# Layer-2 probabilities from a second score product with the keys on the partitions, with an order written out for each engine

## The reference

```python
# layer 0
alpha = max((x@wq) @ (x@wk).T, 0) * (adj != 0);  alpha = softmax(alpha, axis=1)
y = layernorm(x + alpha @ (x@weight))
# layer 1, per head
q, k, v = heads(y@Wq + bq), heads(y@Wk + bk), heads(y@Wv + bv)
scores = where(adj == 0, -inf, q @ k.T / sqrt(32))
attn = softmax(scores, axis=-1)
out = layernorm(y + (attn @ v) @ Wo + bo)
```

## Time and profile before

| what | value |
|---|---|
| median of three runs | 2967.55 us |
| the profiled execution, its own time | 2969.42 us |
| its span (first to last instruction) | 2967.6 us |
| mean granted PE clock | 0.992 |
| PE busy | 2902.2 us, 98% |
| DVE busy | 2365.3 us, 80% |
| ACT busy | 2016.6 us, 68% |
| POOL busy | 582.6 us, 20% |
| DMA, mean busy share of the 16 engines | 23.3% for the kernel's queue |

### The profile page before, as it was taken

How to read it: one execution, slowest core, us unless ns; L and a number is a source line. 1 busy time by engine, 2 the same in 40 slices (tenths; PEclk the granted TensorE clock), 3 DMA queues, 4 the chain that set the end, 5 groups by cost and what they waited for, 6 DMA issues and landing times. The chain is left out here.

```text
span 2967.6 us, 65967 instructions
## 1 busy us (share of the span) xinstructions
PE 2902.2 (98%) x24264; PEld 1775.5 (60%) x24264; DVE 2365.3 (80%) x4627; ACT 2016.6 (68%) x6414; POOL 582.6 (20%) x1289
## 2 busy tenths in 40 slices
PE   7899999999999999999999999999999999999996
PEld 4565666656666656666666666666666666666554
DVE  4588888888888788888788888888888888888886
ACT  3476676666676766676767766767776766776665
POOL 1121122121122121121121221121221211221210
PEclk9999999999999999999999999999999999999997
DMA  3222122222122222122221122221122221222220
GB/s 121 61 72 76 43 56 73 57 76 72 37 65 61 69 76 62 40 72 54 76 76 54 48 72 54 76 76 47 51 76 54 76 76 42 57 71 59 75 53 24
DMA packets 96369, 188.06 MB, mean 63 GB/s; under 512 B 18608, under 2 KB 34992, under 8 KB 96048
## 3 DMA queue, kind: packets, MB, share of 16 engines
q1 hardware_dynamic: 96048, 183.84, 23.3%
HBM read 49.55 MB, written 33.55 MB: 28 GB/s over the span
## 5 line engine op out<-in xcount | busy, mean ns | idle before, releaser
L647 ACT ACTIVATE e<-sm,nmax 128x128 f32<-128x128 f32 x2048 | 791.1, 391 | 27.6 <-DVE nmax L776 25.6
L598 ACT ACTIVATE qk<-front,bqk 128x512 f16<-128x512 f32 x256 | 175.9, 687 | 381.6 <-PE front L429 381.6
L825 POOL TENSOR_TENSOR ln<-ln 128x1 f32<-128x1 f32 x256 | 49.0, 192 | 1890.2 <-DVE ln L804 1496.6
L647 ACT ACTIVATION_READ_ACCUMULATOR e<-sm,nmax 128x1 f32 x2048 | 391.0, 191 | 0.0
L664 DVE SCALAR_TENSOR_TENSOR pT<-pt_bank,pT 128x512 f16<-128x512 f32 x512 | 348.9, 681 | 42.6 <-ACT pT L653 42.1
L653 ACT ACTIVATE pT<-pt_bank 128x512 f16<-128x512 f32 x512 | 302.8, 591 | 103.6 <-PE pt_bank L543 101.6
L776 DVE TENSOR_REDUCE nmax<-sm 128x4 f32<-128x512 f32 x512 | 351.3, 686 | 17.7
L429 PE MATMUL fin_bank<-W_O,oT 128*128 128x512 f16 x1536 | 356.3, 382 | 1.4 <-DVE oT L664 1.4
L429 PE MATMUL front<-W_V,yT 128*128 128x512 f16 x1536 | 354.0, 380 | 0.0
L429 PE MATMUL front<-xT,W_A 128*128 128x512 f16 x1536 | 353.6, 380 | 0.3 <-DVE xT L664 0.3
L429 PE MATMUL front<-yT,W_Q 128*128 128x512 f16 x1536 | 352.2, 379 | 1.6 <-DVE yT L664 1.6
(11 more groups left out here) (111 smaller groups left out, 4482.3 us busy)
## 6 DMA issues: line engine op xcount, KB each, us to landing
q_st<-qk SPq DMA_DIRECT2D x384, 128.0 KB, 2.4
k_st<-qk SPq DMA_DIRECT2D x384, 128.0 KB, 2.4
x_sb<-in_x SPq DMA_DIRECT2D x128, 256.0 KB, 3.4
out_x<-z_sb SPq DMA_DIRECT2D x128, 256.0 KB, 2.5
adj_i<-in_adj SPq DMA_DIRECT2D x32, 256.0 KB, 4.6
y_sb<-in_L_gnn_wq SPq DMA_DIRECT2D x1, 1024.0 KB, 5.6
yb<-in_L_gnn_wk SPq DMA_DIRECT2D x1, 1024.0 KB, 8.1
x_p<-in_L_gnn_weight SPq DMA_DIRECT2D x1, 1024.0 KB, 10.5
```

Source lines behind the costliest of these rows:

```text
L598: i = act.activation(dst, src, ACT.Identity, bias=bias, scale=scale)
L647: act.activation(e1[:, k % 2, h, :], sm[:, k % SM_BUFS, h, :], ACT.Exp, bias=nmax[:, k % SM_BUFS, h:h + 1], accum_out=esum[:, n % 2, head: ...
L825: pool.tensor_tensor(ln[:, 8:9], ln[:, 7:8], ln[:, 8:9], ALU.add).then_inc(moments, 1)
```

## The change

- **Probabilities.** `exp`, `pT` and the transposes of the probabilities go. The scores are computed twice. `S` as before (queries on the partitions) now only serves the row maxima: DVE takes a minimum with a mask of huge values (`smin`) and the negated maxima (`smax`), in two steps. When the four quads of a graph are through, `m` transposes the 16 columns of maxima (one PE transpose f32), ACT and DVE write their HI and LO parts (16 partitions x 128), and SP copies each part into one more row of `q_st` (`m_stack`, 2 DMAs for a graph, rows 96 and 97); `k_st` has a constant in these rows. `T` is the second product, with keys on the partitions, 98 rows: its result is the score minus the row's maximum, already transposed. DVE adds a lift and takes a minimum with a transposed mask; ACT takes the exponential twice over the whole quad, once as f16 (HI) and once as f32; POOL subtracts (`lo`, LO). `PV` follows directly; v has a column of ones beside each head, so its 33rd column is the row sum. `pv_bank` is two banks by halves of eight heads (`o_inv`, `o` in halves).
- **Masks** are made by POOL (`maskb`, `maskT`) instead of DVE. The `mask_size` steps go.
- **x.** ACT and POOL first write the parts of x, then PE transposes these, eight f16 transposes for a job, into a bank read as f16; DVE copies 128x1024 f16 in one instruction. ACT has no part in `xT` any more.
- **Stacking.** The columns of W_Q and W_K are permuted so that q and k come out with head r of a quad interleaved; 12 DMAs of 256 KB a group, three for each operand and pair of quads, and `S` waits for each pair alone.
- **Banks.** `m`, `oT` and `fin` share one bank (`tail`); `adjT` is one job.
- **Order.** Each engine has a list of its own (`ORDER`). `<` is a group's lag, `>` a lead. Dependent DVE instructions are steps of their own, with others between. There is no order of its own for the end: passes −2 to groups+3 run the same list and leave out what does not exist.

```diff
-def pass_order():  ...  (one list for all engines; removed with age, order, drain_order)
+ORDER = {
+    "PE": """
+        fin.0<< yT.1< T.7<< S.12<< yT.2< m.2<< v.0< S.13<< yT.3< PV.5<< PV.6<< xT.0 S.14<< T.8<< xT.1 k.0< S.15<<
+        T.9<< PV.7<< k.1< m.3<< T.10<< PV.8<< q.0< T.11<< PV.9<< q.1< xT.2 T.12<< PV.10<< q.2< T.13<< q.3< oT.1<<
+        T.14<< PV.11<< k.2< PV.12<< xT.3 T.15<< k.3< fin.1<< PV.13<< S.0< t.0 t.1 oT.2<< S.1< t.2 PV.14<< PV.15<< S.2<
+        t.3 S.3< adjT.0 v.1< S.4< m.0< alpha.0 S.5< alpha.1 fin.2<< S.6< T.0< v.2< T.1< S.7< oT.3<< v.3< T.2< z.0 z.1
+        PV.0< S.8< m.1< PV.1< T.3< z.2 z.3 S.9< fin.3<< PV.2< g.0 T.4< PV.3< S.10< g.1 T.5< oT.0< S.11< g.2 g.3 T.6<
+        yT.0 PV.4<
+    """,
...
+    "DVE": """
+        xT.1 o_inv.3<< m.3<< k.0< T.10<< T.11<< k.1< z_bn.0<< o.3<< q.0< z_ag.0<< T.12<< o_inv.4<< xT.2 q.1< T.13<<
+        o.4<< q.2< T.14<< q.3< xT.3 oT.1<< k.2< o_inv.5<< T.15<< k.3< o.5<< z1.1<< smin.0< z_bn.1<< adj01.0 smin.1<
+        t.0 o_inv.6<< t.1 z_ag.1<< o.6<< oT.2<< o_inv.7<< smax.0< smax.1< smin.2< t.2 smax.2< smin.3< t.3 smax.3<
+        adjT.0 o.7<< smin.4< m.0< v.1< smin.5< alpha.0 smax.4< a_max.0 alpha.1 a_max.1 smax.5< z1.2<< p_inv.0 T.0<
+        p_invp.0 p_inv.1 smin.6< p_invp.1 z_bn.2<< smax.6< z_ag.2<< p_lo.0 p_lo.1 smin.7< p_lo.2 T.1< p_lo.3 v.2<
+        oT.3<< smax.7< T.2< v.3< z.0 smin.8< m.1< T.3< z.1 z.2 z.3 smin.9< o_inv.0< smax.8< o.0< smax.9< z1.3<< y.0
...
+    """,
+    "SP": """
+        stack_k.1<< store.0<<< store.1<<< m_stack.0<< m_stack.1<< load.0 load.1 load.2 store.2<<< load.3 m_stack.2<<
+        load_adj.0 m_stack.3<< store.3<<< stack_k.0< stack_q.0< stack_q.1<
+    """,
+}
# PE
                 if what == "xT":
+                        pe.wait_ge(xhi_ready, (g + 1) * GB)
+                        pe.wait_ge(xlo_ready, (g + 1) * GB)
+                    parts = bank[:, :].bitcast(F16)
+                    for part in (HI, LO):
+                        for n in range(GB):
+                            mm = pe.transpose(parts[:, at:at + P], x_p[:, part, n, k * P:(k + 1) * P], ident16[:, :])
-                elif what == "pT":
-                    for h in range(4):
-                        mm = pe.transpose(pt_bank[:, h * P:(h + 1) * P], e1[:, k % 2, h, :], ident[:, :])
+                elif what == "m":
+                    pe.wait_ge(nmax_ready, g * STEPS + QUADS * (k + 1))
+                    pe.transpose(tail[:, 0:P], nmax[:, k % 2, :], ident[:, :]).then_inc(m_full, 1)
+                elif what == "T":
+                    if quad == 0:
+                        pe.wait_ge(m_stacked[n], (g + 1) * 32)
+                    wait(pe, u_ready, g * STEPS + k)
+                    for h in range(4):
+                        mm = pe.matmul(t_bank[:, h * P:(h + 1) * P], k_st[0:ROWS, h, quad, n * P:(n + 1) * P],
+                                       q_st[0:ROWS, h, quad, n * P:(n + 1) * P], start=True, stop=True)
# ACT
-                    for h in range(4):
-                        act.activation(e1[:, k % 2, h, :], sm[:, k % SM_BUFS, h, :], ACT.Exp,
-                                       bias=nmax[:, k % SM_BUFS, h:h + 1], accum_out=esum[:, n % 2, head:head + 1])
-                    act.activation(pT[:, k % 2, HI, :], pt_bank[:, :], ACT.Copy, scale=P1_SCALE)
+                    act.activation(pT[:, k % 2, HI, :], src, ACT.Exp, scale=SCORE_UNSCALE).then_inc(phi_ready, 1)
+                    act.activation(e32[:, k % 2, :], src, ACT.Exp, scale=SCORE_UNSCALE).then_inc(e_ready, 1)
+                elif what == "m":
+                    act.activation(mT[:, k % 2, HI, :], tail[0:HEADS, 0:P], ACT.Copy, scale=M_SCALE)
# DVE
-                    lo_part(pT[:, k % 2, LO, :], pt_bank[:, :], P1_SCALE, pT[:, k % 2, HI, :])
+                elif what == "T":
+                    dve.scalar_tensor_tensor(out=u[:, k % 2, :, :], in0=t_bank[...], scalar=LIFT,
+                                             in1=maskT[:, n, :]..., op0=ALU.add, op1=ALU.min).then_inc(u_ready, 1)
+                elif what == "xT":
+                    dve.tensor_copy(xT[:, :, k, :], front_bank(what, k, g)[:, :].bitcast(F16)...)
# POOL
+                elif what == "lo":
+                    pool.tensor_tensor(pT[:, k % 2, LO, :], e32[:, k % 2, :], pT[:, k % 2, HI, :], ALU.subtract)
# SP
-                for r in range(4):
                     for row, part in enumerate(parts):
-                        sp.dma_start(dst[row * DH:(row + 1) * DH, r, :, :], qk[r * DH:(r + 1) * DH, n, part, :, :])
+                        sp.dma_start(dst[row * DH:(row + 1) * DH, :, pair, :], qk[:, n, part, pair, :])
+                elif what == "m_stack":
+                    for part, ready in ((HI, mhi_ready), (LO, mlo_ready)):
+                        sp.wait_ge(ready, g * GB + k + 1)
+                        sp.dma_start(q_st[MAXROWS + part:MAXROWS + part + 1, :, :, k * P:(k + 1) * P],
+                                     mT[:, k % 2, part, :]).then_inc(m_stacked[k], 16)
```

More of the change, by code:

```diff
@@ L100, in age @@
[L100 to L127, removed]
-    out = []
[L129 to L134, removed]
-    return out
@@ L139 @@
[L139 to L158, removed]
+MROW = 65504.0
+M_SCALE = 1.0 / MROW
@@ new lines, with steps_of, program @@
+FRONT = ("xT", "adjT", "t", "alpha", "z", "g", "yT", "q", "k", "v")
+BY_ACT = ("t", "z", "yT", "q", "k", "v")
+TAIL = ("m", "oT", "fin")
+def steps_of(engine):
+    out = []
+    for word in ORDER[engine].split():
+        name = word.rstrip("<>")
+        what, k = name.split(".")
+        out.append((what, int(k), word.count("<") - word.count(">")))
+    return out
+def program(engine, groups):
+    out = []
+    for p in range(-2, groups + 4):
+        for what, k, age in steps_of(engine):
+            if 0 <= p - age < groups:
+                out.append((what, k, p - age))
+    return out
@@ L263, in graph_layers @@
         y_ready = sem("y_ready")
[L264 to L268, removed]
+        maskb_ready = sem("maskb_ready")
+        maskT_ready = sem("maskT_ready")
+        stacked = [[sem(f"stacked_{n}{half}") for half in range(2)] for n in "qk"]
         yb_ready = sem("yb_ready")
@@ L272, in graph_layers @@
         nmax_ready = sem("nmax_ready")
[L273 to L276, removed]
+        mhi_ready = sem("mhi_ready")
+        m_full = sem("m_full")
+        mlo_ready = sem("mlo_ready")
+        m_stacked = [sem(f"m_stacked{n}") for n in range(GB)]
+        t_full = sem("t_full")
+        u_ready = sem("u_ready")
+        phi_ready = sem("phi_ready")
+        e_ready = sem("e_ready")
+        p_ready = sem("p_ready")
         pv_done = sem("pv_done")
@@ L294, in wait @@
         def wait(eng, s, value):
-            if not (isinstance(value, int) and value <= 0):
+            if value > 0:
                 eng.wait_ge(s, value)
[L299 to L309, removed]
@@ L408, in _ @@
[L408 to L420 removed]
+            for n, b in enumerate((bq, bk)):
+                for t in range(KT):
+                    sp.dma_start(bqk[:, n, t:t + 1], b[t * P:(t + 1) * P].rearrange("(r d) -> d r", r=4),
+                                 allow_slow_non_contiguous=True).then_inc(bias_loaded, 16)
@@ L425, in _, with split_product @@
         def _(pe):
-            def split_product(bank, left, right, k, of, last_inc=None):
+            def split_product(bank, left, right, k, of):
                 for n, (a, b) in enumerate([(HI, HI), (HI, LO), (LO, HI)]):
@@ L478, in step @@
                     if k == 0:
-                        pe.wait_ge(f_free, jobs_done(g, "xT", KT - 1))
-                    bank = bank_for(g)
+                        for n in range(KT):
+                            wait_freed(pe, "xT", n, g)
                     for t in range(KT):
@@ L485, in step @@
                     if k == 0:
-                        pe.wait_ge(f_free, jobs_done(g, "t", KT - 1))
-                    bank = bank_for(g)
+                        for n in range(KT):
+                            wait_freed(pe, "t", n, g)
                     for n in range(2):
@@ L502, in step @@
                     if k == 0:
-                        pe.wait_ge(f_free, jobs_done(g, "z", KT - 1))
-                    bank = bank_for(g)
+                        for n in range(KT):
+                            wait_freed(pe, "z", n, g)
                     for t in range(KT):
@@ L515, in step @@
                     if k == 0:
-                        pe.wait_ge(f_free, jobs_done(g, "yT", GB - 1))
-                    bank = bank_for(g)
+                        for n in range(GB):
+                            wait_freed(pe, "yT", n, g)
                     w = W_Q if what == "q" else W_K
@@ L712, in step @@
-                    dve.wait_ge(f_free, jobs_done(g, what, k))
+                    wait_freed(dve, "adjT", 0, g)
+                    dve.scalar_tensor_tensor(out=two(e0[:, pair, :]), in0=front_bank(what, k, g)[:, 0:2 * P], scalar=0.0,
```

(4 more changed lines are left out.)

646 lines of the change are left out of this document (330 added, 316 removed), and 18 rows, old and new, of the table LATE_ATTENTION.

## The result

| | before | after |
|---|---|---|
| median | 2968.16 us (2967.03 to 2969.31, 4 runs) | 3056.33 us (3055.15 to 3076.05, 4 runs) |
| span of the profiled execution | 2967.6 us | 3054.1 us |
| start to the first product of `t` | 39.2 us | 52.5 us |
| from there to the end of the last k projection | 2843.2 us | 2911.2 us |
| from there to the end | 85.2 us | 90.4 us |

The ratio is 1.0313, interval 1.0271 to 1.0354: the changed kernel is slower by 3%, where 2882 us was forecast and 2943 was the upper end of the range. Of the 86.5 us between the spans, 68.0 arose in the middle, 13.3 at the start and 5.2 at the end.

The account below looks back on a forecast made before the run. PE was taken as the bound, before and after. From the median 2967.55 us, −87 for 31 steady passes, +6 at the start and −5 at the end gave 2881.5, say 2882 us; range 2857 to 2943.

Parts of the forecast that it names:

- rival 4: In `xT`: f16 transposes cost the f32 price, +1.7 us a pass, 54 us in all, 2936 us; chance 0.05.
- 0.9 us of gaps: PE's idle time allowed per steady pass, in place of 0.4, for three tight hand-overs; turned −3.3 into −2.8 us.
- The sum: Whole kernel: −87 us over 31 steady passes, +6 at the start, −5 at the end, giving 2882 us.
- The tightest place: Row maxima to `T`: 3.5 to 4.0 us needed, against 4.5 us of PE work behind m.2.
- Rival 1: Late maxima: small copies land after 4.6 us for 2.4, m.2 1.6 us late; +61 us, 2943 us; chance 0.15.
- rival 3: POOL's subtractions lock DVE out of shared SBUF ports, lengthening the softmax chain; 2898 us, at worst 3009; chance 0.07.
- The start: Before the first `t` product: x's split 5.3 us later, bias loads 0 to 2 us; +6 us taken.
- Rival 2: Lost clock: `T` waits 2.93 us each pass, then PE slows by 1.4 us; 3000 us, chance 0.09.

Follow-up runs that it names:

- C: Copies alone, no other part of the kernel: 3.1 MB as 12 x 256 KB, 128 partitions to 32, runs of 2 KB, as in the kernel after; 26.6 us.
- e2: Kernel after with `T` reading weights instead of the stacked operands, so stacking waits for `S.15` alone; 2866.71 us, ratio to before 0.9653.
- v1: Whole change, but W_Q and W_K unpermuted and stacking in 24 copies of 128 KB a group, 32 partitions to 32; 2848.72 us, ratio to before 0.9598.
- e1: Kernel after, each operand's third stacking copies cut to 32 KB from the second group on; 2855.18 us, ratio to before 0.9619.
- b1: Kernel before with only the new stacking copies, 12 x 256 KB from 128 partitions onto 32, W_Q and W_K unpermuted; 3209.49 us, ratio 1.0812.
- B: Copies alone, 3.1 MB in the kernel before's form, 32 partitions to 32, but in runs of 2 KB; 17.14 us.
- A: Copies alone, 3.1 MB as 24 x 128 KB, 32 partitions to 32, runs of 4 KB, as in the kernel before; 16.93 us.
- O: Copies alone, 3.1 MB from 32 partitions onto 8; 55 GB/s.
- H: Copies alone, 3.1 MB as 48 x 64 KB, 32 partitions to 32, runs of 2 KB; 31.7 us.

## Why the prediction was wrong

**The step that failed** is the one that says "Stacking: the same 3 MB in 12 issues for 24, at 0.59, −7 us on SP; S.0 now waits for the first pair only, and the pair behind k.3 has 12 us until S.2." It took bytes and issues as the price and kept the landing of 2.2 to 2.4 us of rows that were copies from 32 partitions to 32. The new copies have another shape, 128 to 32, for which the trace had no row, and the sum put nothing for that. They move 118 GB/s alone (C), and in the kernel the median one lands after 8.4 us (k) and 11.2 us (q). There was a second miss: `T` reads the stacked operands, which moved the start of the stacking behind `T.13`, and this wait on SP was not listed. The two work together: copies from 128 partitions onto 32 with a lead of 17.7 us (e2) or copies from 32 to 32 with 12.3 (v1) do almost no harm, 128 onto 32 with 12.5 does.

**What it costs:** 3.7 + 1.4 us of waiting and 1.7 at the lower clock in the period shown. Against v1, which lacks it: 192 us in the middle (2911.2 against 2718.9), and 7 of the 90.4 us at the end, where v1 has 83.1. The prediction had called a period over 88.5 us the sign of being wrong; it was 92.6.

**The other steps**, with the stacking out of the way (v1):
- *PE.* −3.3 us a pass was forecast; the period fell from 89.6 to 85.6 (1480.31 to 1565.87 in v1), −4.0, of which the 0.4 us of gaps are one part. T at 0.22 start to start and `xT`'s eight f16 transposes at 0.44 (1558.33 to 1558.77) were right (both read in after), so rival 4 was not. The 0.9 us of gaps that I allowed in each pass never came: that is 28 of the 37 us by which v1's middle gained more than forecast, and 0.3 us more off PE's work in each pass is the rest.
- *The sum.* For middle, start and end I had −87, +6 and −5; v1 has −124.3, +4.5 and −2.1. With good copies the change is worth 119.5 us, not 86, all of the difference from the middle.
- *The tightest place*, maxima to `T`: 2.8 us of waiting in the whole kernel after, 1.2 in v1. Rival 1 was false.
- *The lock* (rival 3) is there, but cost PE nothing. The typical durations stayed (POOL's subtraction 1158 ns, p0's low part 347), because the two hardly ever meet: in after one of the 128 low parts begins inside a subtraction, and it takes 1170 ns. In v1 (and likewise in e1 and e2) the cast of the mask to f16, which takes 0.41 us in after, begins 0.15 us behind a subtraction in 29 of 32 passes and then takes 1.28 us, until just behind the subtraction's end. After, then v1:
```profile
148.57 1.16 POOL L801 TENSOR_TENSOR pT<-e,pT 128x512 f16<-128x512 f32 x1 [50.16 <-ACT e L585]
148.71 1.17 DVE L598 SCALAR_TENSOR_TENSOR p<-e,st,p 128x128 f16<-128x128 f32 x1
...
1481.64 1.16 POOL L790 TENSOR_TENSOR pT<-e,pT 128x512 f16<-128x512 f32 x1 [4.30 <-ACT e L575]
1481.79 1.28 DVE L627 TENSOR_SCALAR adj<-adj_i 128x512 f16<-128x512 int32 x1
```
  The Trainium skill (SBUF — State Buffer, section "SBUF: two separate sides") states that whichever of the two engines starts first holds the shared ports for its whole instruction, when VectorE's has two SBUF inputs as p0's low part has. The trace agrees: 1170 ns for the one that met, 347 on average. Rival 3 thus had a real mechanism. The softmax chain did not meet it in the steady part, and v1's 0.87 us a pass on DVE were covered, since that period has no gap on PE.
- *DVE* 69.0 us for 73: the copy of 1024 f16 columns takes 0.675 us and not 1.1, which is 1.7 of the 4 us; the rest was not traced. *ACT* 45.5 for "near 40": the new exponentials cost what was said (623 and 617 ns), but I subtracted durations of instructions that overlap on the engine; before, one exponential with its read took 0.39 us from start to start (1506.44 to 1506.83 on ACT) and not 391 + 191 ns, so 64 of them were 25 us and not 37, and ACT fell by 17 us a pass and not 29. *POOL* 38.1 for 39.
- *The start*, +13 for +6. PE waited 7.2 us for `o_sb`, which holds the bias of v, and the small bias loads are not the cause: DVE wrote `o_sb` at 35.60 us, 0.2 us behind the split of the last weight, with no idle time for a load; in v1 at 28.32. What was late is the split of W_Q and W_K into HI and LO. With the permuted columns ACT needs 4.82 us for W_Q's HI part and DVE 4.77 for its LO part; without (v1) 1.93 and 2.28. The prediction put this at nothing. After, then v1:
```profile
16.87 4.82 ACT L526 ACTIVATE W_Q<-v_p 128x2048 f16<-128x2048 f32 x1
...
16.85 1.93 ACT L516 ACTIVATE W_Q<-v_p 128x2048 f16<-128x2048 f32 x1
```
  v1, with the columns unpermuted, starts `t` at 43.7, where I had said 45.

**Rival 2 had the right mechanism at the wrong place.** It priced a wait on a DMA in every pass at 2.93 + 1.4 us; measured in the period shown were 3.66 and 1.7, and 1.4 on `S.2`. I looked for it at `T`, which had the new small copies, and not at the stacking, which already stood behind the row of 2.93 us that I took the price from the earlier trace rows. So it got 0.09 and stood outside the range.

## What to carry to other kernels

Count what a DMA does by its shape on both sides, not by bytes and issues: where a copy inside SBUF takes more partitions than it fills, measure that form alone before building on it. When an operand gets a new reader, write down from when its buffer may now be overwritten, and compare the lead that remains with the landing time. And where a kernel lives on an unbroken PE, count more for a wait than its own length: here 145.3 us of waits that v1 lacks came with 62.8 us more of PE's busy time, and b1's 172.3 us with 68.3, though not behind every single wait.

## What the runs showed of the hardware

- Copies from SBUF to SBUF, 3.1 MB each time: 128 to 128 partitions 295 GB/s; 32 to 32, 64 to 64 and 32 to 128 181 to 191; 128 to 64, 128 to 32 and 64 to 32 110 to 121; 32 to 8 55 GB/s. Runs of 2 KB instead of 4 cost nothing to speak of (B 17.14 us, A 16.93).
- Why taking many partitions onto few is slow was not settled. The Trainium skill (SBUF — State Buffer, "Door 1: The DMA port swizzle") gives 27.2 GB/s for each port, and by its table 8 partitions reach two ports, an estimate of 54 GB/s; the 55 of form O agrees, though O also had the DMA engines only 48% busy, against 96% in C, so it may be slow for another reason. The page's table counts eight ports for 32 partitions as for 64, and by the ports of the destination alone C would equal A; the 118 against 186 GB/s say otherwise. The cause stays open.
- SP's issue of a 128 KB copy took 0.63 us (15.20 for 24) in form A alone and 0.82 in v1's period; 48 copies of 64 KB (H) take 31.7 us, 0.66 each, with the DMA engines only 41% busy: there the issues are the bound.
- After a wait of 3.66 us PE was granted 0.54 of full speed (2.4 GHz) for the next 2.1 us and 0.76 over 7.0, although it had been busy before; the 24 matmuls of t.0 and t.1 took 6.87 us in place of 5.18. After a wait of 2.54 us they took 6.87 in one period and 5.19 in another.
- Two VectorE instructions that began while GpSimd's 128x512 subtraction ran lasted until just behind its end: p0's low part (128x128, two SBUF inputs) 1.17 us for 0.35 in after, the cast from int32 to f16 (128x512) 1.28 us for 0.41 in v1. `T`'s minimum with the mask, which reads a PSUM bank and one mask, was not held: 0.69 us in 193 such cases, 0.67 elsewhere (after).
- Writing W_Q's HI part with permuted columns took ACT 4.82 us for 1.93, and its LO part DVE 4.77 for 2.28.
